# VectorE takes over the weight-block sums of a fused cross-attention and expert layer, and its queue is put in another order

## The reference, cut to what matters

```
scores = einsum('ntd,ed->nte', layernorm(x), gate_w);  probs = softmax(scores)
g, m = top_k(probs.transpose(0, 2, 1), k)       # 512 tokens of each expert and sequence
h = gelu(x[m] @ w1[e]) @ w2[e]                  # 512 -> 2048 -> 512
out[m] += g * h
```

## Time and profile before

| | us |
|---|---|
| median of 3 runs | 1783.54 (1780.68 to 1787.02) |
| the profiled execution | 1785.64 |
| its span, first to last instruction | 1783.9 |
| TensorE busy | 1724.9 |
| VectorE busy | 1164.5 |
| ScalarE busy | 807.7 |
| GpSimd busy | 477.3 |

### The profile page before, as it was taken

One profiled execution on the slowest core, in us unless ns is written; L12 is line 12 of the kernel. 1 busy time (PEld: TensorE's weight loads), 2 busy tenths in 40 slices (PEclk: granted clock), 3 DMA queues, 4 the chain that ended last, 5 costly groups with the idle time before them and its releaser, 6 DMA issues.

```text
span 1783.9 us, 22943 instructions
## 1 busy us (share of the span) xinstructions
PE 1724.9 (97%) x8502; PEld 1435.8 (80%) x8502; DVE 1164.5 (65%) x1946; ACT 807.7 (45%) x1786; POOL 477.3 (27%) x451
## 2 busy tenths in 40 slices
PE   7999999899999999999999999999999999999997
PEld 6799988687787878888878887888788878887886
DVE  5455477677766665766686668666766676676663
ACT  4556656363333333544454445445444544454442
POOL 2122222210113020431254216312621361143112
PEclk9999999899999999999999999999999999999999
DMA  3233335242335242431152114312331341133003
GB/s 124 71 131 106 116 111 187 83 154 95 88 123 144 95 139 98 107 106 48 48 95 95 48 54 89 103 63 62 71 105 48 71 103 63 48 73 69 24 1 47
DMA packets 76125, 156.30 MB, mean 88 GB/s; under 512 B 4436, under 2 KB 4590, under 8 KB 76023
## 3 DMA queue, kind: packets, MB, share of 16 engines
q1 hardware_dynamic: 61687, 121.38, 19.7%
q0 software_dynamic: 14336, 33.56, 10.4%
HBM read 121.37 MB, written 33.55 MB: 87 GB/s over the span
## 4 chain that ended last, share of the span: by engine, by line
PE 77%; DVE 9%; ACT 7%; issue 6%; DMA 1%; POOL 1%; SPq 0%; DVEq 0%; ACTq 0%; POOLq 0%
PE ps L1746 7%; PE ps L1748 7%; PE ps L1747 7%; PE ps L1768 7%; PE ps L1769 7%; PE ps L1770 7%; PE ps L1652 3%; PE ps L1654 3%; PE ps L1653 3%; PE ps L1639 3%; PE ps L1641 3%; PE ps L955 3%; PE ps L1640 3%; PE ps L956 3%; PE ps L957 3%
## 5 line engine op out<-in xcount | busy, mean ns | idle before, releaser
L1768 PE MATMUL ps<-v2h,hhS 128*128 128x512 f32 x768 | 302.6, 394 | 4.9 <-DVE YS L1546 3.4
L1769 PE MATMUL ps<-v2l,hhS 128*128 128x512 f32 x768 | 299.1, 390 | 0.0
L1770 PE MATMUL ps<-v2h,hlS 128*128 128x512 f32 x768 | 299.0, 389 | 0.0
L1746 PE MATMUL ps<-Th,Wh 128*128 128x512 f32 x672 | 264.0, 393 | 13.0 <-ACT u L1355 9.2
L1748 PE MATMUL ps<-Th,Wl 128*128 128x512 f32 x672 | 263.1, 392 | 0.0
L1747 PE MATMUL ps<-Tl,Wh 128*128 128x512 f32 x672 | 263.1, 392 | 0.0
L1529 DVE TENSOR_TENSOR hlS<-hfS,hhS 128x512 fp32r<-128x512 f32 x192 | 172.3, 906 | 73.9 <-ACT hfS L1346 73.9
L1199 POOL TENSOR_TENSOR Wf<-w_raw 128x512 f32<-128x512 f32 x24 | 31.2, 1299 | 613.7 <-PE ps L1748 613.7
L1327 ACT ACTIVATE v2h<-w_raw 128x512 fp32r<-128x512 f32 x96 | 57.6, 624 | 273.7 <-PE ps L1770 273.7
L1546 DVE SCALAR_TENSOR_TENSOR YS<-ps,tok_gate,YS 128x512 f32<-128x512 f32 x144 | 105.8, 745 | 113.7 <-PE ps L1770 113.7
L1768 PEld LDWEIGHTS ps<-v2h,hhS 128*128 128x128 f32 x768 | 144.2, 188 | 41.4 <-DVE YS L1546 8.4
(11 more groups left out here) (212 smaller groups left out, 3576.7 us busy)
## 6 DMA issues: line engine op xcount, KB each, us to landing
w_raw<-in_L_ffn_w_dram SPq DMA_DIRECT2D x80, 1024.0 KB, 5.2
XB<-in_x_dram SPq DMA_DIRECT2D x16, 512.0 KB, 4.0
XR<-in_x_dram SPq DMA_DIRECT2D x16, 512.0 KB, 3.5
out_dram<-X SPq DMA_DIRECT2D x16, 512.0 KB, 4.7
xn_rows<-XN SPq DMA_DIRECT2D x16, 512.0 KB, 5.4
w_raw<-in_L_xattn_Wq_dram SPq DMA_DIRECT2D x1, 1024.0 KB, 9.6
w_raw<-in_L_xattn_Wo_dram SPq DMA_DIRECT2D x1, 1024.0 KB, 12.9
w_raw<-in_L_xattn_Wk_dram SPq DMA_DIRECT2D x1, 768.0 KB, 6.5
```

Source lines behind the costliest of these rows:

```text
L1746: nc.tensor.matmul(ps[:, bank, :], wh, th, start=(idx in OPENS and k == 0), stop=False, **go_on)
L1768: nc.tensor.matmul(ps[:, bank, :], th, wh, start=(t == 0), stop=False)
L1769: nc.tensor.matmul(ps[:, bank, :], th, wl, start=False, stop=False)
L1770: last = nc.tensor.matmul(ps[:, bank, :], tl, wh, start=False, stop=(t == GF - 1))
```

## The change

It has four parts. (1) The four weight sums leave GpSimd and become `w_sum` on VectorE, with the same operands and waits: two of them after `low` 5, two after `low` 7; those of group 0 in slot 60. (2) VectorE's queue in a group: both `c11` first, then `w2_low` 0 and 1, `low` 0 and 1, `w2_low` 2 and 3; after the products one `w_low`, then `evict` 0 and 1, then two, `evict` 2, then the last four. In the last group of an expert the last `w_low` now stands ahead of `t_stage` 1, and `t_stage` 3 ahead of `evict` 5. (3) The thresholds live in a fourth entry of two alternating `kept` tiles, so that `dve_narrow` has two operations instead of three. (4) The round of slot 17 moves to slot 18, the count of the round of slot 16 from TensorE's slot 17 to 18; the choice and all that follows it comes one slot later; the lookups' slots are chosen so that VectorE writes `hot` in no slot 0 or 1 of a column.

```diff
-            nc.vector.scalar_tensor_tensor(out=kept[:], in0=counts, scalar=float(CAP), in1=cand[:],
+            nc.vector.scalar_tensor_tensor(out=kept[n % 2][:, :, 0:CAND], in0=counts, scalar=float(CAP), in1=cand[:],
                                            op0=ALU.is_ge, op1=ALU.mult).then_inc(s_kept, 1)
             dve.wait_ge(s_kept, n)
-            nc.vector.tensor_reduce(best[:], kept[:], AX.X, ALU.max).then_inc(s_best, 1)
-            dve.wait_ge(s_best, n)
-            nc.vector.tensor_tensor(thr[:], thr[:], best[:], ALU.max).then_inc(s_thr, 1)
+            nc.vector.tensor_reduce(threshold(b, k + 1), kept[n % 2][:], AX.X, ALU.max).then_inc(s_thr, 1)
...
-        ROUNDS_AT = tuple(range(3, 3 + ROUNDS))
+        ROUNDS_AT = tuple(range(3, KF + 1)) + (KF + 2,)
+        COUNTS_AT = tuple(q + 2 if q == KF else q + 1 for q in ROUNDS_AT)
...
-        HOT_AT = {1: 1, **{m: VALS_AT + 1 + 2 * (m - 2) for m in range(2, len(LOOKUPS))}}
-        FOUND_AT = {1: 3, **{m: VALS_AT + 2 + 2 * (m - 2) for m in range(2, len(LOOKUPS))}}
+        HOTS = [q for q in range(VALS_AT + 1, 3 * KF + 4) if q % KF == KF - 1 or (q % 2 == 0 and q % KF > 1)]
+        HOT_AT = {1: 1, **{m: HOTS[m - 2] for m in range(2, len(LOOKUPS))}}
+        FOUND_AT = {1: 3, **{m: q + 1 for m, q in HOT_AT.items() if m > 1}}
...
-            w_sums(0)
...
-                if n + 1 < NG:
-                    w_sums(n + 1)
...
+                if n == T_AT[3]:
+                    for idx in (SS1, SS2, SS4, SS3):
+                        w_sum(0, idx)
...
+            def w_sum(n, idx):
+                a11, a12, a21, a22 = (w_block(n, i) for i in (A11, A12, -1, A22))
+                if idx == SS1:
+                    dve.wait_ge(s_raw1[n % 2], 16 * (n // 2 + 1))
+                    if n:
+                        dve.wait_ge(s_prod, NU * n)
+                    one, two, op = a21, a22, ALU.add
+                elif idx == SS2:
+                    dve.wait_ge(s_sum, 4 * n + 1)
+                    one, two, op = Wf[:, SS1], a11, ALU.subtract
+                elif idx == SS4:
+                    dve.wait_ge(s_sum, 4 * n + 2)
+                    one, two, op = a12, Wf[:, SS2], ALU.subtract
+                else:
+                    one, two, op = a11, a21, ALU.subtract
+                nc.vector.tensor_tensor(Wf[:, idx], one, two, op).then_inc(s_sum, 1)
...
+                c11(n, 0)
+                c11(n, 1)
                 w2_low(n, (0, 1))
-                c11(n, 0)
-                w2_low(n, (2,))
                 low(n, 0)
-                c11(n, 1)
-                w2_low(n, (3,))
                 low(n, 1)
+                w2_low(n, (2, 3))
...
-                for m in range(5, len(HIDDEN)):
-                    low(n, m)
-                more, last = n + 1 < NG, g == G - 1 and x + 1 < NS
+                low(n, 5)
                 if more:
-                    for idx in W_ORDER[0:3]:
-                        w_low(n + 1, idx)
+                    w_sum(n + 1, SS1)
+                    w_sum(n + 1, SS2)
+                low(n, 6)
+                low(n, 7)
+                if more:
+                    w_sum(n + 1, SS4)
+                    w_sum(n + 1, SS3)
+                    w_low(n + 1, A11)
                 evict(n, 0)
                 evict(n, 1)
                 if more:
-                    for idx in W_ORDER[3:5]:
-                        w_low(n + 1, idx)
+                    w_low(n + 1, A12)
+                    w_low(n + 1, A22)
                 if last:
                     t_stage(x + 1, 0, T_BANKS[0])
                 evict(n, 2)
                 if more:
-                    w_low(n + 1, W_ORDER[5])
+                    for idx in W_ORDER[3:]:
+                        w_low(n + 1, idx)
                 if last:
                     t_stage(x + 1, 1, T_BANKS[1])
...
-                if n - 1 in ROUNDS_AT:
-                    pe_round(pe, 1, ROUNDS_AT.index(n - 1))
+                if n in COUNTS_AT:
+                    pe_round(pe, 1, COUNTS_AT.index(n))
```

More of the change, by code:

```diff
@@ L112, in xattn_expert_choice @@
         ps = top.enter_context(nc.psum_tensor("ps", [P, 8, 512], F32))
-        thr = lookup("thr", [P, E])
         cand = lookup("cand", [P, E, CAND])
         bits = lookup("bits", [P, E, CAND])
-        kept = lookup("kept", [P, E, CAND])
-        best = lookup("best", [P, E])
+        kept = [lookup(f"kept{i}", [P, E, CAND + 1]) for i in range(2)]
         hit = lookup("hit", [P, E, CAND, NT], BF16)
@@ L456, in spread, with spread_ap, threshold @@
             return t[:].unsqueeze(2).broadcast_to([P, E, NT])
+        def spread_ap(t):
+            return t.unsqueeze(2).broadcast_to([P, E, NT])
         def each_cand(t):
             return t.unsqueeze(2).broadcast_to([P, E, CAND])
+        def threshold(b, k):
+            return kept[(b * ROUNDS + k + 1) % 2][:, :, CAND]
         def dve_narrow(dve, b, k):
@@ L484, in dve_round @@
                     nc.vector.memset(bits[:, :, m:m + 1], 2.0 ** (32 * m - 95))
-                nc.vector.memset(thr[:], 0.0).then_inc(s_init, 1)
+                nc.vector.memset(threshold(b, 0), 0.0).then_inc(s_init, 1)
                 dve.wait_ge(s_init, b + 1)
@@ L490, in dve_round @@
                 dve.wait_ge(s_bits, n - 1)
-            nc.vector.tensor_tensor(u32(cand), each_cand(u32(thr)), u32(bits), ALU.bitwise_or).then_inc(s_cand, 1)
+            nc.vector.tensor_tensor(u32(cand), each_cand(threshold(b, k).bitcast(U32)), u32(bits), ALU.bitwise_or).then_inc(s_cand, 1)
             dve.wait_ge(s_cand, n)
@@ L510, in dve_masks @@
             dve.wait_ge(s_thr, (b + 1) * ROUNDS)
-            nc.vector.tensor_tensor(tied[:], probs[:, b], spread(thr), ALU.is_equal)
-            link(nc.vector.tensor_tensor(above[:], probs[:, b], spread(thr), ALU.is_gt))
+            nc.vector.tensor_tensor(tied[:], probs[:, b], spread_ap(threshold(b, ROUNDS)), ALU.is_equal)
+            link(nc.vector.tensor_tensor(above[:], probs[:, b], spread_ap(threshold(b, ROUNDS)), ALU.is_gt))
             with nc.allow_low_precision(reason="counts up to 16 are exact in bfloat16"):
@@ L1122, in w_block @@
             return raw[:, k:k + 2, :, half, :]
-        ROUNDS_AT = tuple(range(3, 3 + ROUNDS))
+        ROUNDS_AT = tuple(range(3, KF + 1)) + (KF + 2,)
+        assert len(ROUNDS_AT) == ROUNDS
+        COUNTS_AT = tuple(q + 2 if q == KF else q + 1 for q in ROUNDS_AT)
         CHOICE_AT = ROUNDS_AT[-1] + 1
@@ L1192, in scatter_pair @@
                                         ).then_inc(s_scat, 16)
[L1194 to L1204, removed]
             def t_low(x, j):
@@ L1550, in group @@
                 x, g = divmod(n, G)
+                more, last = n + 1 < NG, g == G - 1 and x + 1 < NS
+                c11(n, 0)
+                c11(n, 1)
                 w2_low(n, (0, 1))
-                c11(n, 0)
-                w2_low(n, (2,))
                 low(n, 0)
-                c11(n, 1)
-                w2_low(n, (3,))
                 low(n, 1)
+                w2_low(n, (2, 3))
                 c22(n, 0)
@@ L1579, in group @@
                 if more:
-                    w_low(n + 1, W_ORDER[5])
+                    for idx in W_ORDER[3:]:
+                        w_low(n + 1, idx)
                 if last:
                     t_stage(x + 1, 1, T_BANKS[1])
-                    evict(n, 3)
+                evict(n, 3)
+                if last:
                     t_stage(x + 1, 2, T_BANKS[0])
-                    evict(n, 4)
-                    evict(n, 5)
+                evict(n, 4)
+                if last:
                     t_stage(x + 1, 3, T_BANKS[1])
[L1588 to L1595, removed]
+                for j in range(5, ND):
+                    evict(n, j)
             for n in range(2):
```

4 lines of the change are left out of this document (2 added, 2 removed).

## The result

The changed kernel takes 1744.06 us, the median of 4 runs (1742.48 to 1744.17), beside 1785.28 (1780.68 to 1787.69) for the kernel before in the same runs. The ratio is 0.977, with a 95% interval of 0.9748 to 0.9793, so the kernel is faster by 41 us. The forecast was 1743.5, the range 1738 to 1756. The profiled execution took 1744.05 us, its span 1742.3.

The account below looks back on a forecast made before the run. TensorE, busy 97% of the span, was taken as the bound, so only its losses could return: 16.7 + 9.5 + 6.3 + 3.2 + 0.9 + 3.5 = 40.1 us, from 1783.54 to 1743.5 us, range 1738 to 1756.

Parts of the forecast that it names:

- The waits of an expert's start: TensorE's two waits when experts 2 to 6 begin go with both `c11` first: 5 x 3.34 = 16.7 us.
- The first rival: GpSimd holds up `c11` through its SBUF input `u1`, so the expert-start waits stay: 1763.5 us, chance 0.09.
- The waits of chunk 3: Late first matmul of chunk 3, three groups per expert, goes with sums on VectorE and evictions forward: 18 x 0.53 = 9.5 us.
- Counts, lookups and their clock: Plain columns: four waits go, 6.3 us, and slow clock behind two lookups, 3.2; shorter threshold rounds help attention counts, 0.9.
- The gather for column 2: Plain columns: its list comes a slot later, using 5.4 of 6.1 us to spare; cost taken as 0, at most 1 us.
- The clock in the groups: Low granted clock in two group stretches, following the expert-start waits, returns to full: 3.5 us, or 0 if it falls anyway.
- (a): TensorE's two waits when an expert begins, behind `w2_low` slowed by GpSimd: 3.34 us lost, five times.
- VectorE late at chunk 3: Rival: strided sums cost 1.78 us each, so `evict` 0 delays chunk 3 by 3.3 us, 18 times: 1812 us, chance 0.03.

Follow-up runs that it names:

- after: The changed kernel with all four parts, against the kernel before: 1744.06 us, ratio 0.977.
- the sums at 1.4: The changed kernel with every weight sum on VectorE made twice, some 1.4 us a sum: 1757.32 us, ratio 0.9842 to the kernel before.
- the sums thrice: The changed kernel with every weight sum on VectorE made three times, some 2.1 us a sum: 1833.02 us, ratio 1.0259 to the kernel before.
- two other kernels: Changed kernel with the old order at a group's head: 1758.03 us; kernel before with sums on VectorE and new tail, old head: 1767.76 us.

## Why the prediction was right

**The waits of an expert's start (16.7).** Right, and by the mechanism named. The head of the group alone gave 20.4 with the clock's return, for 20.2 in the sum. I wrote that the `w2_low` would start 6.2 us after the group's first matmul (919.7 less 913.5), and they started 6.25 after it (906.67 less 900.42). `c22` half 0 came in time. The first rival, GpSimd holding up `c11` as well, falls by the 0.69 us of half 0 in the middle of the block. The Trainium skill (SBUF — State Buffer, "Who interferes with whom") says that a VectorE instruction contends with a GpSimd one that reads SBUF when it has two SBUF inputs, and not when it has at most one. By this rule, the trace agrees: 0.69 for a `c11` here, 6.57 for two `w2_low` before.

**The waits of chunk 3 (9.5).** The size was right. From both `c11` first alone to after are 20.9 us, for 19.9 in the sum of this and the slots. For the seven instructions from the last product to `evict` 0 I had 7 x 0.68 = 4.8 us. The timeline has 4.4 (834.56 to 838.99). What the prediction didn't see is that the two edits that I costed together are each sufficient. It gave the move of the sums a role that it needn't have.

**Counts, lookups and their clock (6.3 + 3.2 + 0.9).** 10.4 foreseen, 11.4 by the ratio. The gather for column 2 cost nothing: its last issue came at 511.03, some 7.4 us ahead of the transposes, and before it took 6.8 us to land. The transposes began at 518.47 without a wait, 0.23 us behind the start of the matmul ahead.

```profile
518.24 0.39 PE L1665 MATMUL ps<-w2h,hl 128*128 128x512 f32 x1
518.47 0.60 PE L1633 MATMUL ps<-ident,XB 128*128 128x128 f32 x4
```

**The clock in the groups (3.5).** It returned in full. The windows show 1.00 where they showed 0.98 and 0.99. That the waits of (a) bring it is shown by the kernel with both `c11` first alone, which has no low clock in the groups. How many of the five waits it follows was luck of the profiled execution: two of five in the kernel before, three of five in the one with the new slots.

**VectorE late at chunk 3.** I put the deciding cost at 1.5 us a sum, for a kernel no faster than before. With the sums at 1.4 the kernel is 13 us over after and still 30 under before, at 2.1 it is 46 over before. The point lies between the two, with the `w_low` at 0.68 in both. The real sum is 0.69, as the shortest `w_low` had said, not 1.78, as its median had.

**What failed** were forecasts for parts alone, on record ahead of two experiments. I took the waits of an expert's start to be untouched by the sums. They depend on how GpSimd's block lies to VectorE's queue, so that moving the sums alone was worth about 20 us, not 9.5. The low clock of the groups, which went with the longest of these waits, is in that 20. In the sum this was hidden, because both `c11` first removes the waits anyway. The parts don't add up: 20 and 20 and 11 would be 51, and all together give 41.

## What to carry to other kernels

Put on VectorE first what the bounding engine waits for soonest, and let subtractions with both inputs in SBUF stand behind it. When two engines slow each other, look at the shortest duration of an instruction: it was the cost alone here (0.68 us), and the median (1.78) showed the company. Try each remedy alone and all but it: the gain of a part alone may hold waits that another part removes as well, and a part of the change may turn out not to be needed.

## What the runs showed that I had not expected

- GpSimd holds VectorE for more than one instruction. A subtraction with two SBUF inputs that began inside a block of four GpSimd subtractions lasted 4.86 to 5.98 us, until the block was over. In the four kernels with a wait between the same four or a chain of small memsets ahead of them, no `w2_low` lasted more than 1.79. The Trainium skill (SBUF — State Buffer, "SBUF: two separate sides") says that whichever of the two starts first has the shared ports for the whole instruction, and the other is blocked. The 1.79 and less agree with that. The 4.86 and more don't, and the measurement decides: VectorE stayed out through the rest of four instructions. Where VectorE was held, GpSimd's records overlap (1.83 to 1.89 us at a spacing of 1.25). The wait between them, the memsets and the idle time all go with records that don't. Whether the overlap is the cause or a sign of it, and why memsets ahead of the block take it away, is open.
- The low clock in the groups came after waits of 1.81 to 1.85 us, behind two of five in the kernel before and three of five in the one with the new slots, and never after the ten of 1.4 to 1.5 us in two other kernels. With the sums thrice it came five times, behind three of the five waits of 2.2 and both of 3.0. In attention it comes behind much shorter ones, as at 299.5 us in the changed kernel, where the last wait ahead of it is one of 0.36 on a count, at 296.23. What decides there stays open.
